# One-head attention over 1024 tokens: float32 score and value products turned into three float16 products each

## The reference, cut to what matters

```python
def _L0_ffn_ref(x, Wq, bq, Wk, bk, Wv, bv, Wo, bo, Wg, bg, W1, b1, W2, b2):
    q = x @ Wq + bq
    k = x @ Wk + bk
    v = x @ Wv + bv
    scale = 1.0 / sqrt(128)
    scores = einsum('bqh,bkh->bqk', q, k) * scale
    attn = softmax(scores, axis=-1)
    a = einsum('bqk,bkh->bqh', attn, v) @ Wo + bo
    x = x + a
    ... # a mixture of 8 experts on the new x
x = x + _L0_attn_ref(xn, ...) + _L0_ffn_ref(xn, ...)
```

## Time and profile before

| | |
|---|---|
| median of 3 runs | 4477.36 us |
| profiled execution, its own time | 4475.59 us |
| its span | 4473.8 us |
| mean granted clock of TensorE | 0.954 of full speed |
| busy in the span | PE 3975.3, DVE 3385.5, ACT 2913.3, POOL 2240.4 us |
| the stage touched | about 1425 to 1620 us, 195 us |
| busy in those 195 us | PE 177.75, DVE 95.94, ACT 76.50, POOL 10.10 us |

### The profile page before, as it was taken

One profiled execution on the slowest core, in us unless ns is written; L12 is line 12 of the kernel. 1 busy time (PEld: TensorE's weight loads), 2 busy tenths in 40 slices (PEclk: granted clock), 3 DMA queues, 4 the chain that ended last, 5 costly groups with the idle time before them and its releaser, 6 DMA issues. The chain is left out here.

```text
span 4473.8 us, 88017 instructions
## 1 busy us (share of the span) xinstructions
PE 3975.3 (89%) x34586; PEld 2227.3 (50%) x34588; DVE 3385.5 (76%) x4741; ACT 2913.3 (65%) x4403; POOL 2240.4 (50%) x1443
## 2 busy tenths in 40 slices
PE   6999999999999979996877777899788877999999
PEld 3666667666666654442111211245677543444443
DVE  6888888888884547767898899565877657878887
ACT  3777777777776449982677777685556644555555
POOL 2888888888886013331121210172566554555555
PEclk7999999999999989996899999898899988999999
DMA  3212212212210011100121100142000224454544
GB/s 84 59 40 59 58 38 59 59 40 58 58 35 16 1 49 48 71 24 29 50 74 43 40 27 16 57 149 72 11 13 15 75 83 115 113 124 116 120 113 108
DMA packets 113913, 270.28 MB, mean 60 GB/s; under 512 B 24276, under 2 KB 36308, under 8 KB 111004
## 3 DMA queue, kind: packets, MB, share of 16 engines
q1 hardware_dynamic: 98084, 223.86, 18.7%
q0 software_dynamic: 15424, 40.89, 2.6%
HBM read 178.10 MB, written 50.81 MB: 51 GB/s over the span
## 5 line engine op out<-in xcount | busy, mean ns | idle before, releaser
L522 POOL TENSOR_TENSOR a_prob_low<-a_prob_whole,a_prob_high 128x1024 f16<-128x1024 f32 x512 | 1085.0, 2131 | 276.7 <-ACT a_prob_high L412 275.6
L496 DVE TENSOR_REDUCE a_part_max<-a_top 128x2 f32<-128x1024 f32 x512 | 626.2, 1223 | 218.7 <-PE a_top L323 212.6
L409 ACT ACTIVATE a_prob_whole<-a_score 128x1024 f32<-128x1024 f32 x512 | 525.2, 1026 | 332.5 <-PE a_score L312 320.5
L976 ACT ACTIVATE a_prob<-a_score 128x512 f32<-128x512 f32 x1024 | 533.1, 603 | 255.9 <-PE a_score L915 255.8
L1009 DVE TENSOR_REDUCE a_part_max<-a_side 128x2 f32<-128x1024 f32 x512 | 595.2, 1220 | 68.3 <-PE a_side L886 68.3
L412 ACT ACTIVATE a_prob_high<-a_score 128x1024 f16<-128x1024 f32 x512 | 521.8, 1019 | 0.0
L311 PE MATMUL a_score<-a_qa,a_ka 128*128 128x256 f16 x2048 | 476.8, 273 | 0.0
L312 PE MATMUL a_score<-a_qb,a_kb 128*128 128x256 f16 x2048 | 476.5, 273 | 0.0
L2185 POOL TENSOR_TENSOR m_lows<-m_scaled,m_high 128x512 f16<-128x512 f32 x264 | 311.2, 1183 | 323.8 <-ACT m_high L2146 322.2
L378 PE MATMUL a_o_ps<-a_v,a_prob_high 128*128 128x65 f16 x4096 | 428.2, 193 | 6.2 <-POOL a_prob_low L522 3.4
L380 PE MATMUL a_o_ps<-a_v,a_prob_high 128*128 128x64 f16 x4096 | 427.0, 194 | 0.0
(11 more groups left out here) (477 smaller groups left out, 10147.8 us busy)
## 6 DMA issues: line engine op xcount, KB each, us to landing
m_gate<-gates SPq DMA_DIRECT2D x264, 256.0 KB, 5.2
a_ka<-a_nat_high_k SPq DMA_DIRECT2D x128, 128.0 KB, 2.4
e_gate<-gates SPq DMA_DIRECT2D x8, 2048.0 KB, 7.2
slots<-in_slots SPq DMA_DIRECT2D x19, 520.0 KB, 4.2
a_qa<-a_nat_high_q SPq DMA_DIRECT2D x64, 128.0 KB, 2.4
a_qa<-a_nat_low_q SPq DMA_DIRECT2D x64, 128.0 KB, 2.4
a_qb<-a_nat_high_q SPq DMA_DIRECT2D x64, 128.0 KB, 2.4
a_kb<-a_nat_low_k SPq DMA_DIRECT2D x64, 128.0 KB, 2.4
```

The source lines that it names most:

```text
L409: eng.activation(prob_whole[:, e % RING, :, :, :], score[:, e % 2, :, :, :], ACT.Exp, scale=scale)
L496: eng.tensor_reduce(part_max[:, i, c, :, qt % 4], top[:, :, :], AX.X, ALU.max).then_inc(max_done, 1)
L522: eng.tensor_tensor(prob_low[:, e % RING, :, :, :], prob_whole[:, e % RING, :, :, :], prob_high[:, e % RING, :, :, :], ALU.subtract).then_ ...
L976: eng.activation(prob[:, e % RING, h, :], score[:, step % SLOTS, :], ACT.Exp).then_inc(exp_done, 1)
```

## The change: what it does

- k, q, v and the turned probabilities are held as two float16 tiles each, a high part (the value rounded) and a low part (what the rounding left). A float32 product becomes three float16 products added up in PSUM: high by high, high by low, low by high. Projections of k, q, v, the turns and the output projection stay float32.
- k: ACT writes `k_whole` in float32 and then `k_high`; POOL subtracts to `k_low`. q: DVE writes `q_whole`, ACT `q_high`, POOL `q_low`. The whole tiles have one buffer each.
- v and the turned probabilities: ACT copies `turned` to the high part (`turned_high`), and DVE subtracts that from `turned` in PSUM to the low part; only this frees `turned`.
- On DVE the low part of turn s-1 stands behind the maximum of scores s and ahead of the normalisation of s.
- Probabilities are multiplied by 1024 in the normalising instruction, which so has two operations, and `mixed` is multiplied by 1/1024.

The core of the diff (allocations, semaphores and renamed arguments are left out):

```diff
@@ TensorE
                     elif what == "scores":
                         if t == 0:
-                            wait_freed(eng, ("k", b))
-                            wait_freed(eng, ("q", b))
+                            eng.wait_ge(split_low, 2 * b + 2)
                         for h in range(2):
-                            mm = eng.matmul(dst[:, h * BANK:(h + 1) * BANK], q[:, b % 2, t * P:(t + 1) * P],
-                                            k[:, b % 2, h * BANK:(h + 1) * BANK], start=True, stop=True)
+                            at = slice(h * BANK, (h + 1) * BANK)
+                            eng.matmul(dst[:, at], q_high[:, b % 2, rows], k_high[:, b % 2, at], start=True, stop=False)
+                            eng.matmul(dst[:, at], q_high[:, b % 2, rows], k_low[:, b % 2, at], start=False, stop=False)
+                            mm = eng.matmul(dst[:, at], q_low[:, b % 2, rows], k_high[:, b % 2, at], start=False, stop=True)
...
                         for kt in range(qts):
-                            mm = eng.matmul(mix[:, t % 4 * P:(t % 4 + 1) * P], v[:, b % 2, kt, :], prob_t[:, n % 2, kt * P:(kt + 1) * P],
-                                            start=(kt == 0), stop=(kt == qts - 1))
+                            to, at = mix[:, t % 4 * P:(t % 4 + 1) * P], slice(kt * P, (kt + 1) * P)
+                            eng.matmul(to, v_high[:, b % 2, kt, :], prob_high[:, n % 2, at], start=(kt == 0), stop=False)
+                            eng.matmul(to, v_high[:, b % 2, kt, :], prob_low[:, n % 2, at], start=False, stop=False)
+                            mm = eng.matmul(to, v_low[:, b % 2, kt, :], prob_high[:, n % 2, at], start=False, stop=(kt == qts - 1))
@@ ScalarE
                     if what == "k":
                         eng.wait_ge(wide_full, slot[job] + 1)
-                        eng.activation(k[:, n % 2, :], wide_ps[:, slot[job] % 2, :], ACT.Identity, bias=bias[:, 1:2]).then_inc(act_freed, 1)
+                        if n:
+                            eng.wait_ge(split_low, 2 * n - 1)
+                        eng.activation(k_whole[:, :], wide_ps[:, slot[job] % 2, :], ACT.Identity, bias=bias[:, 1:2]).then_inc(act_freed, 1)
+                        wait_freed(eng, job)
+                        eng.activation(k_high[:, n % 2, :], k_whole[:, :], ACT.Copy).then_inc(split_high, 1)
+                    elif what == "q":
+                        wait_freed(eng, job)
+                        eng.activation(q_high[:, n % 2, :], q_whole[:, :], ACT.Copy).then_inc(split_high, 1)
...
-                        eng.activation(prob_t[:, n % 2, :], turned[:, :], ACT.Copy).then_inc(turned_read, 1)
+                        eng.activation(prob_high[:, n % 2, :], turned[:, :], ACT.Copy).then_inc(turned_high, 1)
@@ VectorE
-                    eng.tensor_scalar(prob[:, n % 3, :], prob[:, n % 3, :], total[:, n % 4:n % 4 + 1], None, ALU.mult).then_inc(prob_ready, 1)
+                    eng.tensor_scalar(prob[:, n % 3, :], prob[:, n % 3, :], total[:, n % 4:n % 4 + 1], LIFT, ALU.mult, ALU.mult).then_inc(prob_ready, 1)
...
-                    elif what == "turn" and n == tiles - 1:
-                        normalise(n)
+                    elif what == "v":
+                        eng.wait_ge(turned_high, turn[job] + 1)
+                        eng.tensor_tensor(v_low[:, n % 2, :, :].rearrange("p a b -> p (a b)"), turned[:, :],
+                                          v_high[:, n % 2, :, :].rearrange("p a b -> p (a b)"), ALU.subtract).then_inc(turned_read, 1)
+                    elif what == "turn":
+                        if n == tiles - 1:
+                            normalise(n)
+                        eng.wait_ge(turned_high, turn[job] + 1)
+                        eng.tensor_tensor(prob_low[:, n % 2, :], turned[:, :], prob_high[:, n % 2, :], ALU.subtract).then_inc(turned_read, 1)
@@ GpSimd
+                def split(b):
+                    eng.wait_ge(split_high, 2 * b + 1)
+                    eng.tensor_tensor(k_low[:, b % 2, :], k_whole[:, :], k_high[:, b % 2, :], ALU.subtract).then_inc(split_low, 1)
+                    eng.wait_ge(split_high, 2 * b + 2)
+                    eng.tensor_tensor(q_low[:, b % 2, :], q_whole[:, :], q_high[:, b % 2, :], ALU.subtract).then_inc(split_low, 1)
+
+                split(0)
                 for n in range(tiles // 4):
+                    if n % 2 == 0 and n // 2 + 1 < B:
+                        split(n // 2 + 1)
```

More of the change, by code:

```diff
@@ L1094, in whole_attention @@
     scale = float(P) ** -0.5
+    LIFT = 1024.0
     def timeline():
@@ L1117, in whole_attention @@
     turn = {job: i for i, job in enumerate(turns)}
-    by_act = [job for job in order if job[0] in ("k", "scores", "v", "turn")]
+    by_act = [job for job in order if job[0] in ("k", "q", "scores", "v", "turn")]
     wide_reads = {}
@@ L1125, in whole_attention @@
         pl = Place(nc, ctx, stage)
-        q = pl.sb("q", [P, 2, N])
-        k = pl.sb("k", [P, 2, N])
-        v = pl.sb("v", [P, 2, qts, P])
+        q_whole = pl.sb("q_whole", [P, N])
+        k_whole = pl.sb("k_whole", [P, N])
+        q_high = pl.sb("q_high", [P, 2, N], F16)
+        q_low = pl.sb("q_low", [P, 2, N], F16)
+        k_high = pl.sb("k_high", [P, 2, N], F16)
+        k_low = pl.sb("k_low", [P, 2, N], F16)
+        v_high = pl.sb("v_high", [P, 2, qts, P], F16)
+        v_low = pl.sb("v_low", [P, 2, qts, P], F16)
         prob = pl.sb("prob", [P, 3, N])
@@ L1131, in whole_attention @@
         total = pl.sb("total", [P, 4])
-        prob_t = pl.sb("prob_t", [P, 2, N])
+        prob_high = pl.sb("prob_high", [P, 2, N], F16)
+        prob_low = pl.sb("prob_low", [P, 2, N], F16)
         mixed = pl.sb("mixed", [P, 2, BANK])
@@ L1145, in whole_attention @@
         turned_full = pl.sem("turned_full")
+        turned_high = pl.sem("turned_high")
         turned_read = pl.sem("turned_read")
+        split_high = pl.sem("split_high")
+        split_low = pl.sem("split_low")
         mixed_tile = pl.sem("mixed_tile")
@@ L1227, in _ @@
                             eng.wait_ge(mixed_tile, qts * (n - 1))
-                        eng.activation(v[:, n % 2, :, :].rearrange("p a b -> p (a b)"), turned[:, :], ACT.Copy).then_inc(turned_read, 1)
+                        eng.activation(v_high[:, n % 2, :, :].rearrange("p a b -> p (a b)"), turned[:, :], ACT.Copy).then_inc(turned_high, 1)
                     elif what == "turn":
@@ L1264, in _ @@
                             eng.wait_ge(proj_full, n // 4 - 1)
-                        eng.tensor_scalar(mixed[:, n // 4 % 2, :], mix[:, :], bias[:, 2:3], None, ALU.add).then_inc(mixed_half, 1)
+                        eng.tensor_scalar(mixed[:, n // 4 % 2, :], mix[:, :], 1.0 / LIFT, bias[:, 2:3], ALU.mult, ALU.add).then_inc(mixed_half, 1)
                     elif what == "proj":
```

5 lines of the change are left out of this document (4 added, 1 removed).

## The result

The kernel after takes 4516.43 us (median of four runs, 4513.84 to 4522.23), the kernel before, on the same chip, 4476.32 us (four runs, 4473.0 to 4477.38). The ratio is 1.0093, with a 95% interval of 1.0078 to 1.0108: slower by 0.93%, 40 us. The forecast of 4528 is 11.6 us too high, the range 4508 to 4554 held the time, and of the single numbers on record rival A's 4520, which had a chance of 0.28, is the nearest.

A forecast was written before the change was run, and what follows sets the result against it. PE set a plain tile before; afterwards a closed DVE-ACT chain of 5.61 us would. Loop, head and tail +39.4, POOL's hold 8.1 and clock 5 gave +52.5 on 4475.6: forecast 4528 us, range 4508 to 4554.

The forecast's parts named there:

- rival A: Negation in the tiles: POOL does not hold it, so the 8.1 us drop out; 4520 us, chance 0.28.
- closed chain of seven terms: Plain tile: negation, exponential, copy, low part, reciprocal, product, maximum follow one another across DVE and ACT; 5.61 us.
- PE's part: Plain tile: float16 products need 3.5 us of PE instead of 4.3, 26 us over 32 tiles if PE set the pace.
- The loop: First to last maximum: 205.1 us against 170.8, +34.3.
- the negation beside POOL: 128x1 negation held by POOL's new k and q subtractions: bounds 0 and 8.1 us, 8.1 taken.
- The clock: PE's granted clock falling after gaps: costs between 0 and 10.6 us over the stage, 5 taken.
- The head: Stage before the first maximum: splitting q and k makes the first maximum 2.8 us later.
- The tail: After the last maximum: 13.4 us to the end of the last residual sum against 11.1, +2.3.
- rival C: Clock stays low through most of the stage, PE sets the pace at 6.9 us a tile; 4562 us, chance 0.08.
- B: Normalising product with two operations runs at half the pace, adding 16.4 us and giving back 7.3; 4537 us, chance 0.10.
- D: Faster: the low part does not close the chain and PE's 26 us come out; 4455 us, chance 0.05.
- E: No change: chain is 4.4 us because the low part from PSUM takes far less than from SBUF; chance 0.04.

The follow-up runs named there:

- e4: Kernel after, with ACT copying the turned tile s-1 before it takes the exponential of s; 4483.58 us, ratio 1.0019 to the kernel before.
- e3: Kernel after, with DVE normalising tile s before it makes the low part of turn s-1; 4491.85 us, ratio 1.0043 to the kernel before.
- e6: Kernel after, with a fourth product, low by low, added to scores and values; 4518.15 us, ratio 1.0095 to the kernel before.
- e5: Kernel after without the low part of the turned probabilities, the second values product reading the high part again; 4472.71 us, ratio 0.9996 to the kernel before.
- e8: e1 with DVE taking the residual sum one place later, behind the next product; 4460.27 us, ratio 0.9971 to the kernel before.
- e1: Kernel after with only the scores in float16, values back to one float32 product; 4471.85 us, ratio 0.9995 to the kernel before.
- e11: Kernel after, with DVE taking the residual sum one place later, behind the next product; 4513.76 us, ratio 1.0083 to the kernel before.

## Why the prediction was right, and where it was off

**The mechanism: right.** The closed chain of seven terms was summed to 5.61 and measured 5.59 (5.58 in the step behind a v or projection step). Low part 1.224 (taken 1.22), though no row had 1024 columns from PSUM; product with two operations 0.75 beside nothing; the longest waits are the two that were named. e4 shows the cause by moving one link, e3 by moving another; e6 shows that PE at the full clock is not in it.

**PE's part: right.** In the kernel after, float16 products with 512 columns start 0.216 apart (1446.08, 1446.30, 1446.51) and those with 128 columns 0.055 (1468.43, 1468.48, 1468.54), as in the earlier trace rows. In e5, with the same products, PE was busy for 3.47 us of a plain step, the 3.5 of the sum.

**The loop: right.** 205.1 was summed without POOL's hold and the clock; 206.3 was measured, with 1.5 us of the clock in it (one v step of 12.77 in place of 11.71, one projection step of 7.74 in place of 7.28). The k steps took 0.1 more than a plain one, "just in time". The v term was 4.3 each; a v step holds the residual and its product too, 11.71 - 5.59 - 0.67 - 1.04 = 4.4. The timeline of the kernel after shows its links in order, PE's v only behind the low part of the turn:

```profile
1478.49 1.23 DVE L1290 TENSOR_TENSOR b_prob_low<-b_turned,b_prob_high 128x1024 f16<-128x1024 f32 x1 [2.19 <-ACT b_prob_high L1254]
...
1479.77 2.05 PE L1190 MATMUL b_turned<-all_kept_w_b,all_xn_t 128*128 128x128 f32 x16 [0.65 <-DVE b_prob_low L1290]
...
1481.86 1.02 ACT L1249 ACTIVATE b_v_high<-b_turned 128x1024 f16<-128x1024 f32 x1 [3.40 <-PE b_turned L1190]
...
1482.91 1.22 DVE L1284 TENSOR_TENSOR b_v_low<-b_turned,b_v_high 128x1024 f16<-128x1024 f32 x1 [3.20 <-ACT b_v_high L1249]
...
1484.90 1.78 DVE L1263 TENSOR_SCALAR b_prob<-b_prob,b_total 128x1024 f32<-128x1024 f32 x1
```

**The mis-sized term: the negation beside POOL, 8.1 taken, 0 measured.** Its bounds were 0 and 8.1, and I took the upper end from the nearest row, the 128x8 instruction of the earlier trace rows; that this row speaks for one column is the step that failed. The timeline of the kernel after at POOL's two new subtractions:

```profile
1468.44 2.13 POOL L1306 TENSOR_TENSOR b_k_low<-b_k_whole,b_k_high 128x1024 f16<-128x1024 f32 x1 [28.75 <-ACT b_k_high L1235]
...
1468.71 0.15 DVE L1281 TENSOR_SCALAR b_top<-b_top 128x1 f32<-128x1 f32 x1
...
1475.29 2.13 POOL L1308 TENSOR_TENSOR b_q_low<-b_q_whole,b_q_high 128x1024 f16<-128x1024 f32 x1 [4.72 <-ACT b_q_high L1238]
...
1476.15 0.15 DVE L1281 TENSOR_SCALAR b_top<-b_top 128x1 f32<-128x1 f32 x1
```

Both negations lie wholly inside a subtraction of POOL and take 0.15, as do all six that start beside one; over all 32 the mean is 0.153 and none is above 0.155. Rival A was right; this term is most of what the forecast was too high. The Trainium skill (VectorE: DVE Perf Modes, Mode 2×_2P) says that in this mode the access is split in half and each port streams one half. The rows agree with the reading that a single column has no second half, and so no need of the port that POOL holds; the page does not say it of one column, and no run here tried two, so the reason stays a reading and only the 0.15 is shown. Four columns are not free of it: in the kernel before a 128x4 copy in SBUF (L2245, at 3840.09) took 0.82 us beside a subtraction of POOL, and the other three of that line 0.17.

**The clock: 5 taken, about 4 measured.** It stood at its lower level (0.50) when the stage began, fell six times up to the last maximum and once in the tail, each time while PE had work and with a gap ahead of it. In the plain steps it cost nothing: in the step that holds the fall from 1451.3 to 1454.7 PE was busy for 5.36 us in place of 3.73, and the step kept its 5.59. It cost 1.5 in the loop, as above, 0.9 in the head and about 1.7 in the tail. The 5 was picked between 0 and 10.6, so that it came out near is in part luck: no k step met a fall, for which up to 1.7 each had been counted, and one of the three v steps and one projection step paid. **The head** grew by 3.7 and not 2.8. The timeline of the kernel after, against the earlier trace rows:

```profile
1428.65 6.43 PE L1183 MATMUL b_wide<-all_xn_t,all_kept_w_b 128*128 128x512 f32 x8 [1.05 <-PEq L268]
...
1437.56 2.12 POOL L1308 TENSOR_TENSOR b_q_low<-b_q_whole,b_q_high 128x1024 f16<-128x1024 f32 x1 [0.71 <-ACT b_q_high L1238]
...
1439.83 0.38 PE L1199 MATMUL b_wide<-b_k_high,b_q_high 128*128 128x512 f16 x1 [2.97 <-POOL b_q_low L1308]
...
1441.45 1.23 DVE L1279 TENSOR_REDUCE b_top<-b_wide 128x1 f32<-128x1024 f32 x1 [1.80 <-PE b_wide L1201]
```

The eight projection records took 6.43 us; in the kernel before 5.56, as the lower clock at their start ended sooner. Those 0.9 us are the excess. They are not tied to the projection: in e8 it took 5.65, but then the score products came at the lower clock, 0.43 apart (1437.52, 1437.95, 1438.38 in its timeline), and the head was 12.83 all the same. **The tail** grew by 4.0 and not 2.3. Its timeline in the kernel after, against the earlier trace rows, and the window:

```profile
1653.48 1.97 PE L1207 MATMUL b_turned<-all_kept_ident,b_prob 128*128 128x128 f32 x8 [2.29 <-DVE b_prob L1263]
1655.49 1.02 ACT L1254 ACTIVATE b_prob_high<-b_turned 128x1024 f16<-128x1024 f32 x1 [4.18 <-PE b_turned L1207]
...
1660.15 0.75 DVE L1295 TENSOR_SCALAR b_mixed<-b_mix,all_kept_bias_b 128x512 f32<-128x512 f32 x1 [2.38 <-PE b_mix L1217]
```

```profile
1655.00:1659.00 4.00, 4.00 (x39) 3.86 (x38) 1.23 (x1) 1.02 (x1) 0.00 (x0) 0.50 0.00 0
```

The turns took 1.97 where they take 1.10, and the values behind them ran at 0.50. (The 1.7 is the excess over the forecast of the tail; e6, whose clock stayed up in its tail, took 13.91 there with 0.44 more of PE, which bears out the 13.4.) The Trainium skill (TensorE: Matmul & The Clock Gate, Part 1: The HAM clock gate) says that activity lifts the lower clock. The trace agrees: in five of the six falls up to the last maximum PE was busy all the while, each fall ended by itself, and the stage's mean stayed at 0.92, so rival C did not come.

**The other rivals.** B (half pace): the product took 0.753 where POOL was silent. D (faster) and E (same) needed a chain shorter than 4.4; on DVE's and ACT's orders as written it was 5.6. e4 shows what D would have needed, and that even then the time is 4483.6: in the orders as written the 26 us of PE were not to be had, because v, q and the projection steps do not run on PE's sum. This the prediction did not see: it priced D at 4455, and e1, where PE does set the plain step, and e5, where it nearly does, measured 4471.9 and 4472.7.

**In sum**, stage without POOL's hold: 34.3 + 2.8 + 2.3 + 5 = 44.4 forecast, 43.2 measured. Of the 13.1 us by which the forecast missed the profiled execution (4528.1 against 4515.05) 8.1 are the negation, 1.2 the stage's other terms, and the rest, nearly 4, lies outside the stage, where nothing was forecast. The median of the runs is 1.4 above the profiled execution, which makes the miss 11.7.

## What to carry to other kernels

Before adding a step that reads one engine's result on another, write both in-order queues as one loop and add up the closed chain per iteration: if it is longer than the busiest engine's sum, making that engine faster gives nothing, and the cure is the order, not the work. Here exchanging two neighbours on ACT gave back 33 of 40 us; the work of the added instruction kept another 11 in that order (e4 against e5). And look for the instruction that waits for the latest result while others behind it in its queue are ready (here the residual sum); moving it one place gave 0.15% by itself, while the whole change, in the best order that was tried, added nothing to that which could be measured.

## What the runs showed of the hardware that was not expected

- A 128x1 `tensor_scalar` in SBUF is not held by a POOL subtraction that runs beside it (0.15 us in all six cases), where a 128x8 one in the earlier trace rows took 1.49 until POOL's end and a 128x4 copy 0.82.
- A subtraction of 1024 columns with one input in PSUM and a float16 output takes 1.224 us on DVE, the same as with both inputs in SBUF.
- The granted clock fell to the lower of its two levels (0.50) in stretches in which PE was busy all the time (1475.4 to 1478.7: 3.30 of 3.30 us busy, clock 0.52), so the fall comes later than the gap ahead of it, and its price depends on what room PE has then: nothing in a plain step of the kernel after, 0.83 us in one of e6, 1.65 us in each of two k steps of e11. In e11 it fell thirteen times up to the last maximum, where the kernel after has six, and in its loop only those two k steps paid.
